# The attention's sixteen batches written out, x loaded batch by batch, the second layer's weights and the bias fold moved into the first batch, GpSimd's first norm ahead of its clearing

## The reference, cut to what matters

```python
    x = x + _L1_xattn_ref(_layernorm(x, axis=-1), ctx_1024, ctx_1024, mask_SxS2_bk0, L1_xattn_Wq, ...)
    x = x + _L1_ffn_ref(_layernorm(x, axis=-1), L1_ffn_Wq, L1_ffn_bq, ...)
# in _L1_xattn_ref, 16 heads of 16 features
        logits = jnp.einsum('bhqd,bhkd->bhqk', q, k) * SCALE
        masked = jnp.where(mask, logits, -1000000000.0)
        weights = jax.nn.softmax(masked, axis=-1)
...
        return out @ Wo.T
# in _L1_ffn_ref
        x = x + _layernorm(_attention(x, Wq, bq, Wk, bk, Wv, bv, Wo, bo), ln1_g, ln1_b)
        x = x + _layernorm(_moe(x, gate_w, gate_b, W1, b1, W2, b2), ln2_g, ln2_b)
```

## Time and profile before

| | |
|---|---|
| runs, median (lowest to highest) | 2591.42 us (2586.67 to 2592.35), 3 runs |
| the profiled execution's own time | 2591.02 us |
| its span in the profile | 2589.3 us |
| TensorE busy, matmuls | 2222.8 us (86%) |
| VectorE, ScalarE, GpSimd busy | 50%, 39%, 27% |
| mean granted TensorE clock | 0.93 of full speed |

### The profile page before, as it was taken

The page is one execution under the profiler, slowest core; times in us unless marked ns, Lnnn a source line. Parts: engine busy times, 40 slices in busy tenths (PEclk is TensorE's granted clock), DMA queues, the critical chain, the costliest instruction groups (busy, mean ns, idle before and its releaser), DMA issues. The chain is left out here.

```text
span 2589.3 us, 37681 instructions
## 1 busy us (share of the span) xinstructions
PE 2222.8 (86%) x10760; PEld 1242.3 (48%) x10760; DVE 1304.4 (50%) x3466; ACT 1015.8 (39%) x1836; POOL 710.9 (27%) x718
## 2 busy tenths in 40 slices
PE   6878399984999898999999999999727999999990
PEld 2565266651333332334333333333326888888880
DVE  5556533313777576676777676677472111111115
ACT  2223112210555454555565555556502223233222
POOL 4114223323111001112123331323112334334335
PEclk9988699995999899999999999899958999999995
DMA  4327434427232232222234423234005666666664
GB/s 160 116 94 234 147 111 104 112 33 178 35 59 47 48 60 51 35 50 36 31 45 59 59 39 45 43 51 59 9 8 167 189 174 190 189 174 190 190 187 134
DMA packets 198682, 255.26 MB, mean 99 GB/s; under 512 B 21168, under 2 KB 176816, under 8 KB 196464
## 3 DMA queue, kind: packets, MB, share of 16 engines
q1 hardware_dynamic: 177968, 224.89, 34.1%
q0 software_dynamic: 20544, 28.33, 6.1%
HBM read 161.95 MB, written 52.67 MB: 83 GB/s over the span
## 5 line engine op out<-in xcount | busy, mean ns | idle before, releaser
L1782 ACT ACTIVATE att_prob<-att_ps 128x512 f32<-128x512 f32 x1024 | 599.5, 598 | 526.1 <-PE att_ps L1643 283.2
L1929 DVE CUSTOM_DVE_ANT_0 att_junk<-att_pm,bias 128x512 bf16<-128x512 f32 x512 | 344.2, 687 | 182.6 <-PE att_pm L1626 178.2
L1640 PE MATMUL att_ps<-att_qstack,att_kstack 99*128 99x512 bf16 x1024 | 397.7, 389 | 35.9 <-issue 26.2
L1925 DVE TENSOR_REDUCE att_tops<-att_pm 128x1 f32<-128x512 f32 x512 | 341.3, 684 | 159.0 <-PE att_pm L1626 154.0
L1626 PE MATMUL att_pm<-att_kstack,att_qstack 96*128 96x512 bf16 x1024 | 401.5, 393 | 12.2 <-DVE att_tops L1925 4.9
L1199 PE MATMUL exL_po<-exL_w,exL_hid 128*128 128x256 f32 x1696 | 379.4, 382 | 17.7 <-DVE exL_ys L1266 8.9
L1183 PE MATMUL exL_ph<-exL_xgT,exL_w 128*128 128x256 f32 (+2 forms) x1504 | 387.9, 413 | 5.7 <-ACT exL_hid L1216 3.0
L1216 ACT ACTIVATE exL_hid<-exL_ph,exL_b 128x256 f32<-128x256 f32 (+2 forms) x376 | 186.7, 501 | 439.4 <-PE exL_ph L1183 422.6
L1199 PEld LDWEIGHTS exL_po<-exL_w,exL_hid 128*128 128x128 f32 x1696 | 317.9, 190 | 70.7 <-issue 14.4
L1183 PEld LDWEIGHTS exL_ph<-exL_xgT,exL_w 128*128 128x128 f32 x1504 | 269.0, 191 | 109.9 <-issue 59.8
L1149 POOL DMA_INDIRECT sum<-exL_ys,exL_put x106 | 175.1, 1651 | 420.5 <-DVE exL_ys L1266 248.0
(11 more groups left out here) (310 smaller groups left out, 2403.2 us busy)
## 6 DMA issues: line engine op xcount, KB each, us to landing
exL_w<-in_L_W SPq DMA_DIRECT2D x94, 1024.0 KB, 5.1
att_qstack<-att_q SPq DMA_DIRECT2D x192, 128.0 KB, 5.9
kstack<-pick_k SPq DMA_DIRECT2D x48, 256.0 KB, 3.2
att_kstack<-kstack SPq DMA_DIRECT2D x16, 768.0 KB, 7.5
att_kstack<-att_k SPq DMA_DIRECT2D x96, 128.0 KB, 4.6
exL_b<-in_L_b SPq DMA_DIRECT2D x47, 128.0 KB, 5.3
values<-pick_vals SPq DMA_DIRECT2D x8, 574.0 KB, 4.5
att_vals<-values SPq DMA_DIRECT2D x8, 574.0 KB, 3.8
```

The source lines that it names most:

```text
L1640: mm = pe.matmul(ps[i % 2][:], stack["k"][par][0:KR + 3, h, kc * P:(kc + 1) * P], stack["q"][par][0:KR + 3, h, :], start=True, stop=me.self_)
L1782: act.activation(prob[i % PROBS][:], ps[i % 2][:], ACT.Exp, scale=SCALE).then_inc(s["p_ready"], 1)
L1925: ins = dve.tensor_reduce(tops[g % 2][:, t, j:j + 1], pm[i % TOPS][:], AX.X, ALU.max)
L1929: ins = dve.tensor_tensor_reduce(junk[:, i % TOPS, :], pm[i % TOPS][:], G["bias"][0][:, t, :], 1.0, -BIG / 2, ALU.add, ALU.max, tops[g % 2 ...
```

## The change

- `run`: both loops are gone; a Python loop writes all 16 batches out, for all five engines. The bookkeeping of register bases goes with them, and so does the separate empty instruction that a chained operation had behind a computed wait.
- x: `load_x(0)` at the start, `load_x(1)` in `before`, and each cross batch loads the piece for the batch after the next, behind its values.
- `load_weights` moves from `before` to batch 0, behind its value load and x piece.
- The bias fold becomes a job of batch 0 at step 40, in bank `a`: VectorE spreads `bv` into `uT` in group 2 at step 5, TensorE multiplies, ScalarE copies the result, VectorE adds it to `bo` in group 2 at step 13.
- The first fill of the query stack: SyncE issues three of six copies of each half, ScalarE the other three, behind its projections' copies.
- GpSimd in `before`: the norm first; the clearing of stack 0 then waits for the normalised x.

```diff
+    if prev_self is None:
+        jobs += [(40, "a", "fold0+")]
...
-            batch(Where(0, False, None, False), 0)
-            with eng.Fori(0, (B - 2) // 2) as pair:
-                batch(Where(pair * 2 + 1, False, False, False), 1)
-                batch(Where(pair * 2 + 2, False, False, False), 0)
-            batch(Where(B - 1, False, False, True), 1)
-            batch(Where(0, True, False, True), 0)
-            with eng.Fori(0, (B - 2) // 2) as pair:
-                batch(Where(pair * 2 + 1, True, True, True), 1)
-                batch(Where(pair * 2 + 2, True, True, True), 0)
-            last = Where(B - 1, True, True, None)
-            batch(last, 1)
+            for rows in range(B):
+                batch(Where(rows, False, False if rows else None, rows == B - 1), rows % 2)
+            for rows in range(B):
+                last = Where(rows, True, rows > 0, None if rows == B - 1 else True)
+                batch(last, rows % 2)
...
-                        for k, part in enumerate(terms):
+                        for k, part in enumerate(terms[0:QUEUED] if w.start else terms):
...
                     load_values(w.next, 0)
-                    load_x(slice(CB, NC), "x_rest")
-                    load_weights()
+                    load_x(1)
                     fill(w, 0, 0)
                     fill(w, 0, 1)
...
                         load_values(w.next, 1 - par)
+                        if w.next.rows + 1 < B:
+                            load_x(w.next.rows + 1)
+                    if w.first:
+                        load_weights()
...
+                    elif kind == "fold":
+                        pe.wait_ge(s["loaded"], past(16 * LOADS))
+                        pe.wait_ge(s["spread"], past(1))
+                        for m in range(DC):
+                            ins = pe.matmul(pj["a"][:, 0:D], uT[:, m, 0:P], wo[True][:, m, :],
+                                            start=m == 0, stop=m == DC - 1)
...
+                    for o in range(DC):
+
+                        act.wait_ge(s[f"cut{o}"], past(1))
+                        for k in range(QUEUED, len(Q_TERMS)):
+                            act.dma_start(stack["q"][0][16 * k:16 * k + 16, o * HC:(o + 1) * HC, :],
+                                          parts["q"][Q_TERMS[k]][:, o, :]).then_inc(s[f"stacked{o}"], 16)
...
-                    if i:
-                        pool.wait_ge(s["cut1"], past(1))
+                    pool.wait_ge(s["cut1" if i else "xn_ready"], past(1))
...
                 def before(w):
+                    norm(w.next)
                     clear(0)
-                    norm(w.next)
...
+                            if w.first and (g, n) == (2, 5):
+                                dve.wait_ge(s["loaded"], past(16 * LOADS))
+                                dve.tensor_copy(uT[:, :, 0:P], bv[:].unsqueeze(2).broadcast_to([P, DC, P])
+                                                ).then_inc(s["spread"], 1)
+                            if w.first and (g, n) == (2, 13):
+                                dve.wait_ge(s["free_a"], past(w.index("a", "fold0+") + 1))
+                                dve.tensor_tensor(bo[:], bo[:], uT[:, 0, D:2 * D], ALU.add).then_inc(s["folded"], 1)
+                                dve.wait_ge(s["folded"], past(1))
```

More of the change, by code:

```diff
@@ L1418, in attention @@
                  "m_ps", "m_done", "neg_ready", "neg_in", "s_ps", "p_ready", "pv_done", "o_saved", "job_a", "job_d",
-                 "free_a", "free_d", "vchain", "pchain", "cleared", "vals_in", "keys_in0", "keys_in1", "x_first", "x_rest",
+                 "free_a", "free_d", "vchain", "pchain", "cleared", "vals_in", "keys_in0", "keys_in1", "x_in0", "x_in1",
                  "y_stats", "y_rstd", "yn_ready", "u_ready", "u_added", "rows_stored", "shift_ready", "rexp_ready",
-                 "xn_kept", "spread", "fold_ps", "folded"]
+                 "xn_kept", "spread", "folded"]
         s = {n: st.sem(n) for n in names}
@@ L1424, in attention @@
         PER = NG * ROUND
-        LOADS = 12
+        LOADS, QUEUED = 12, 3
         STACKED = len(Q_TERMS) * 16
@@ L1458, in _, with load_x @@
             def _(sp):
-                def load_x(here, name):
+                def load_x(rows):
+                    here = slice(rows * CB, (rows + 1) * CB)
                     sp.dma_start(X[:, here, :], G["sum0"][0][0:N, :].rearrange("(c p) d -> p c d", p=P)[:, here, :]
-                                 ).then_inc(s[name], 16)
-                load_x(slice(0, CB), "x_first")
+                                 ).then_inc(s[f"x_in{rows % 2}"], 16)
+                load_x(0)
                 st.set_semaphores(sp)
@@ L1651, in value_quad @@
                         pe.wait_ge(s["vals_in"], past((of.rows + 1) * 16))
-                    if kc == 0 and first_batch(of) and g == 0:
-                        pe.wait_ge(s["folded"], past(1))
-                    elif kc == 0:
+                    if kc == 0 and not (first_batch(of) and g == 0):
                         pe.wait_ge(s["o_saved"], past(of.number * NG + g))
@@ L1666, in before @@
                         job(w.next, "a", name, w.index("a", name))
[L1668 to L1673, removed]
                     for n in range(ROUND):
@@ L1746, in job @@
                         ins = act.copy(attT[:, i, :], pj["a"][:])
+                    elif kind == "fold":
+                        ins = act.copy(uT[:, 0, D:2 * D], pj["a"][:, 0:D])
                     else:
@@ L1817, in keep @@
                     pool.wait_ge(s["xn_ready"], past(of.number + 1))
+                    if isinstance(of.rows, int) and of.rows == 0:
+                        pool.wait_ge(s["loaded"], past(16 * LOADS))
                     if not (isinstance(of.rows, int) and of.rows < 2):
@@ L1852, in before @@
                     clear(1)
-                    pool.wait_ge(s["loaded"], past(16 * LOADS))
-                PPER = {False: 6 + 1, True: 12 + 1 + 2}
-                start = {}
                 def batch(w, par):
[L1859 to L1863, removed]
                     if not w.last:
@@ L1873, in batch @@
                         keep(w.next, 1 - par)
[L1874 to L1877, removed]
                 def behind(last, after):
@@ L1891, in norm_chunk @@
                     of = w.next
-                    if not of.self_ and isinstance(of.rows, int) and t == 0:
-                        dve.wait_ge(s["x_rest" if of.rows else "x_first"], past(16))
+                    if not of.self_ and t == 0:
+                        dve.wait_ge(s[f"x_in{of.rows % 2}"], past((of.rows // 2 + 1) * 16))
                     if of.self_ and t == 0:
@@ L2032, in before @@
                         apply_chunk(w, t)
[L2034 to L2039, removed]
                     for n in range(ROUND):
@@ L2048, in before @@
                         cut_maxima(w.next, 1, 1, k)
-                VPER = {False: 5 * NG + 1, True: 4 * NG + 1 + 6}
-                start = {}
                 def batch(w, par):
[L2054 to L2058, removed]
                     for g in range(NG):
@@ L2088, in batch @@
                                 max_step(w.next, g - 2, n)
[L2089 to L2092, removed]
                 def behind(last, after):
```

## The result

The changed kernel takes **2545.32 us** (median of 4 runs, 2542.74 to 2550.92) against 2591.89 (4 runs, 2586.67 to 2593.3) for the kernel before on the same chip: ratio 0.9827, interval 0.9804 to 0.985, so 46.6 us less. The forecast was 2543, 2531 to 2556. The profiled execution took 2543.31 us, with a span of 2541.5 and a mean granted clock of 0.94.

A forecast was written before the change was run, and what follows sets the result against it. TensorE was taken to bound the kernel, idling at loop jumps; -25.9 - 7.2 - 2.4 - 4.0 - 10.4 + 1.1 = -48.8 from 2591.0 gave 2542.2, set at 2543 us for the runs' median, range 2531 to 2556.

The forecast's parts named there:

- Cross jumps, -25.9: Cross attention: without jumps to the loop's head, two long stretches lose 13.0 and 12.9 us.
- register work, -2.4: Six cross batches: waits no longer compute their values, 0.4 us saved per batch, 2.4 in all.
- Rival E: Heads of cross batches 1 to 7: fetching written-out code during key loads starves TensorE, 10.6 us each; chance 0.07.
- -7.2 for the jumps: Self attention: removing the loop's two jumps saves 4.3 and 2.9 us.
- 0 for register work: Self batches: no gain from dropped register work, since their length is not set by issue.
- -4.0 for dips: Self stage: two half-clock stretches without a jump cost 8.0 us together; half taken as gained, bounds 0 and -8.0.
- the 2.9 us that I gave to the second self jump: Second self jump's stretch: 6.9 us too long, 4.0 given to a clock dip and 2.9 to the jump.
- The opening, -10.4: Start of the attention: first query copies land at about 614.4, so top products start there instead of at 624.82.
- The weights in batch 0, 0: Batch 0: second-layer weight loads fit SyncE's free queue time behind the value load, so moving them costs nothing.
- The fold, +1.1: Batch 0: the bias fold's products lengthen a full TensorE by 1.1 us, between 0.8 and 2.0.
- Rival B: Self stage: clock dips all stay or one comes elsewhere, 0 or +4.0 us, total 2547 to 2551; chance 0.15.
- the prediction's own signs of being wrong: TensorE idle at key-load heads, batch 0's fill late, or more than two half-clock stretches in self batches.

The follow-up runs named there:

- experiment 3: Kernel before, loops kept, with the next cross batch's keys loaded later, behind that batch's first negatives; 2583.5 us (one run).
- experiment 9: Changed kernel with the gate's logits made in four pieces (steps 57 to 60) instead of two; 2535.78 us, ratio 0.979.
- experiments 1 to 3: Kernel before with: both loops written out (2552.13 us); six batches in each loop's body, one pass (2551.86 us); cross key load issued later (2583.5 us).
- experiment 8: The changed kernel measured once more with no edit; 2548.29 us, ratio 0.9841.
- experiment 10: Changed kernel with logits in four pieces and, in self batches, the next batch's first negatives issued by ScalarE's queue; 2535.95 us, ratio 0.9789.

## Why the prediction was right

**Cross jumps, -25.9, and register work, -2.4.** Shown. Six stretches of before add up to 25.9 (jumps) and 6 x 0.42 = 2.5 (73.71 to 73.29) more than six of after; with the fold's 0.8 in batch 0 this is the 27.6 of the table. Rival E, a fetch that starves at heads with key loads, fell: no idle time of a cross head is ended by issue. The Trainium skill ("Runtime: NRT & Kernel Launch", Instruction fetch mechanics) has a taken branch to a target outside the fetched window wait for a fetch and sequential code fetched ahead; both traces agree, 10.6 us against none at the same place. That the jump costs this is shown; that the time goes into the fetch is argued, from queue 8: 3 instruction packets in the 10 us ahead of this head in the kernel before, 1 in the 11 us ahead of it after. Where I said that fetch and key load share the queues, experiment 3 gives the shares: 9 and 4.

**Self, -7.2 for the jumps, 0 for register work, -4.0 for dips.** The sum, -11.2, is what was measured between the marks, but not its parts. Dips did not halve: two long ones lie between the marks in both kernels, and after has a third behind them. That the sum came out all the same is luck. What made up for it is the term I had set to nothing: the undisturbed self batch went from 75.2 (one stretch) to a mean of 74.5 (three), 0.7 each. No run shows what the 0.7 is made of, so my reason, that their length isn't set by issue, doesn't stand. And the 2.9 us that I gave to the second self jump is at most half its own: its 1.49 us of idle time is as long as the 1.49 of a head without a jump, shown above, and a short dip stood behind it, worth about 1.5 by experiment 9. This is its window, kernel before:

```profile
1650.30:1653.70 3.40, 3.40 (x13) 0.74 (x13) 1.54 (x4) 2.19 (x4) 0.00 (x0) 0.50 0.01 5
```

**The opening, -10.4.** Measured -10.2; three other kernels with the old opening (experiments 1 to 3) reach the first top product 38.5 to 38.8 us after x's issue, so the profiled run of before was 1 us late in it and the fair size is about 9. Its steps: the norm 1.1 earlier (1.0 said), the copies 8.9 us from first issue to product (8.45 said, counted from 605.95 where the first cut's end was worked out as 605.85, a slip of 0.1), one queue or two alike. The norm's order is 0.75 to 1.1 us of it and the weights' move 0.6; the rest, by subtraction, is x's load in pieces, which no run changes by itself.

**The weights in batch 0, 0.** The fill was to be issued by about 672; here are SyncE's last weight and its fill, timeline after.

```profile
650.50 0.43 SPq L1486 DMA_DIRECT2D att_gw<-in_L_gate_w  x1
...
658.35 4.13 SPq L1494 DMA_DIRECT2D att_qstack<-att_q  x6
```

7.4 us of cover remained. **The fold, +1.1.** Its group in the kernel after, then the windows of the exponentials of the head group that holds it, after and before:

```profile
L1595 PE MATMUL att_pja<-att_wo,att_uT 128*128 128x256 f32 x4 | 1.0, 379 | 0.0
```

```profile
670.90:688.20 17.30, 9.60 (x17) 1.00 0.34 47
```

```profile
684.40:700.80 16.40, 9.55 (x16) 1.00 0.30 44
```

The two windows differ by one exponential at their edge; from the group's first exponential to the next group's first it is 17.24 against 16.38, so 0.86 us. TensorE's own 1.0 us is as worked out; the batch became 0.8 longer.

**The clock.** The step that was mis-sized is "take half": the dips' term came out at +1.4 for the third one and +3.0 in the tail, instead of -4.0. Rival B had this as "or one comes in another place", and more than two stretches at half clock were among the prediction's own signs of being wrong: there are three. The total hardly shows it, because two things that the prediction did not contain stood against it: the self batches' 3.5 us, and in the profiled execution the 3.4 us ahead of the attention, which are chance. Without the 3.4 that execution would be near 2547, and experiment 8's median is 2548. So the jumps, the register work of the cross batches, the opening and the fold were right by their mechanism; that the total lies within 3 us of the forecast is in part luck.

**What stays open.** Why the granted clock falls at the logits in some batches and not in others that run the same instructions. It goes with how the products are grouped: 12 self batches in the two traces with four pieces have no dip there, while each of the eight other traces without a jump has three to six; whether the grouping does it, or the times that it moves, was not separated. That it depends on when the batches run is argued only: two edits that move the opening by 0.6 to 0.8 us came with six dips, one trace each, and unchanged code moved two of its three. That these dips make the spread of the runs, 8 us for unchanged code, fits their price but wasn't shown, since only one run of each is profiled. Register work in a self batch was not measured apart from the jumps.

## What to carry to other kernels

Cut a trace at one instruction per batch: the stretches show at once what a loop's jump costs (13 us here, with a load beside it) and, by the undisturbed neighbour, what remains without it. A single DMA of 3584 KB held back the next issue of its queue for 16.6 us here, so look for what stands behind a large load: issue the urgent copies first, and cut the load to pieces that come when they are needed. Before crediting an edit with a few us in a long, dense TensorE stage, compare the granted clock's dips in both traces: two edits worth under 1 us each came with three more dips and 14 us here.

## What I had not expected of the hardware

- A jump of the cross loop costs 9 us even with the key load moved away from it (6 of them idle), while the same loop form in the self stage idled 3.8 us once and nothing beyond the usual head wait the other time. Which of the two self jumps idles is not fixed: in experiment 3 the first had the usual 1.5 us, for the negatives' copy, yet its stretch took 77.9 us at full clock, 2.7 more than an undisturbed one; and the second idled for this long.

```profile
1637.95 0.61 PE L1640 MATMUL att_ps<-att_qstack,att_kstack 99*128 99x512 bf16 x1 [4.93 <-issue]
```

- The granted clock falls to 0.50 for 10 us in a stream in which TensorE is busy throughout, where eight products of 8 columns follow 0.76 us of idle time (0.67 in kernels with loops), in 2 to 6 of the self batches, at about 4 us each. With the same products in four pieces instead of two no such dip came, and this version, 2535.78 us, beats both kernels (experiment 10 is level with it).
